# First attention of a two-layer adaLN transformer kernel: three of eight reciprocals taken within their own pair, and half the key evacuations ahead of the last exponentials

## The reference

```python
h = _layernorm(x, axis=-1) * (1 + ca) + sa
x = x + ga * _L0_attn_ref(h, ...)
# inside, 16 heads of 64: q and kv projected and rotated; keys = values = kv
lsim = einsum('bwid,bwjd->bwij', lq, _ln(lkv))   # this window of 128 tokens and the one before
gkv  = _ln(einsum('bnsd,bnsr->bnrd', segments of 16, softmax(segments @ w_proj)))
gsim = einsum('bnd,brd->bnr', q, gkv)            # pooled keys, one per segment of 16 tokens
attn = softmax(concat([gsim, lsim]), axis=-1)    # masked causally
out  = einsum('bwij,bwjd->bwid', attn, v) @ w_out + b_out
```

## Time and profile before

| | us |
|---|---|
| median of 3 runs | 1512.77 |
| the runs | 1503.08, 1512.77, 1513.02 |
| the profiled execution, its own time | 1505.21 |
| its span, first to last instruction | 1503.4 |
| mean granted TensorE clock | 0.888 |
| TensorE / VectorE / ScalarE / GpSimd busy, share of span | 79 / 63 / 55 / 48 % |

### The profile page before, as it was taken

The page is one execution under the profiler, slowest core; times in us unless marked ns, Lnnn a source line. Parts: engine busy times, 40 slices in busy tenths (PEclk is TensorE's granted clock), DMA queues, the critical chain, the costliest instruction groups (busy, mean ns, idle before and its releaser), DMA issues. The chain is left out here.

```text
span 1503.4 us, 29869 instructions
## 1 busy us (share of the span) xinstructions
PE 1185.8 (79%) x9426; PEld 935.1 (62%) x9426; DVE 944.6 (63%) x2134; ACT 826.2 (55%) x2183; POOL 727.6 (48%) x750
## 2 busy tenths in 40 slices
PE   3278989989888982898899899899937987788436
PEld 1155666656666762798899889889923444445335
DVE  4687797887887543745744664664434677777633
ACT  1256776767767772666666666666712443334101
POOL 2647558476485412565566556556644323211223
PEclk7588999899898996999999999999967998999558
DMA  6500000000000004203003000000063455331144
GB/s 185 168 3 3 2 10 3 8 5 7 10 3 8 10 8 160 92 11 126 9 11 123 14 8 10 12 9 11 10 169 86 79 84 110 60 51 21 24 125 149
DMA packets 153550, 74.98 MB, mean 50 GB/s; under 512 B 99992, under 2 KB 144408, under 8 KB 153304
## 3 DMA queue, kind: packets, MB, share of 16 engines
q1 hardware_dynamic: 145464, 64.84, 16.7%
q0 software_dynamic: 3072, 6.31, 1.3%
q10 hardware_dynamic: 4896, 2.36, 0.5%
HBM read 53.20 MB, written 19.76 MB: 49 GB/s over the span
## 5 line engine op out<-in xcount | busy, mean ns | idle before, releaser
L1495 POOL TENSOR_TENSOR hl<-hid,hh 128x256 fp32r<-128x256 f32 x396 | 293.0, 742 | 223.0 <-ACT hh L1472 218.9
L1538 DVE SCALAR_TENSOR_TENSOR hid<-GU,gub,sg 128x256 f32<-128x256 f32 x396 | 190.3, 481 | 194.6 <-ACT sg L1466 115.4
L1366 PE MATMUL GU<-xh,wh 128*128 128x256 f32 x792 | 233.4, 295 | 41.9 <-DVE wl L1514 32.7
L1466 ACT ACTIVATE sg<-GU,gub 128x256 f32<-128x256 f32 x396 | 187.8, 475 | 122.2 <-PE GU L1368 121.6
L1367 PE MATMUL GU<-xl,wh 128*128 128x256 f32 x792 | 225.2, 284 | 0.0
L1368 PE MATMUL GU<-xh,wl 128*128 128x256 f32 x792 | 225.0, 284 | 0.0
L1366 PEld LDWEIGHTS GU<-xh,wh 128*128 128x128 f32 x792 | 151.6, 191 | 52.6 <-issue 27.7
L1472 ACT CAST hh<-hid 128x256 fp32r<-128x256 f32 x396 | 158.1, 399 | 29.8 <-DVE hid L1538 28.8
L1367 PEld LDWEIGHTS GU<-xl,wh 128*128 128x128 f32 x792 | 152.0, 192 | 0.0
L1368 PEld LDWEIGHTS GU<-xh,wl 128*128 128x128 f32 x792 | 151.9, 192 | 0.0
L648 ACT ACTIVATE prob<-prob,rZ 128x272 f32<-128x272 f32 (+1 forms) x256 | 98.9, 462 | 54.0 <-DVE rZ L1029 54.0
(11 more groups left out here) (327 smaller groups left out, 2951.7 us busy)
## 6 DMA issues: line engine op xcount, KB each, us to landing
raw<-in_expert_w SPq DMA_DIRECT2D x4, 2688.0 KB, 12.2
late<-in_w SPq DMA_DIRECT2D x20, 256.0 KB, 6.2
raw<-in_expert_w SPq DMA_DIRECT2D x4, 1152.0 KB, 6.3
list<-zero SPq DMA_DIRECT2D x4, 1024.0 KB, 8.5
modb<-mod_d SPq DMA_DIRECT2D x8, 384.0 KB, 4.1
early<-rel_d SPq DMA_DIRECT2D x1, 3072.0 KB, 13.7
qkv_d<-qkv SPq DMA_DIRECT2D x48, 64.0 KB
early<-in_w SPq DMA_DIRECT2D x12, 256.0 KB, 4.3
```

What stands on the lines that cost most here:

```text
L1366: pe.matmul(out, lhs[0], rhs[0], start=start, stop=False, skip_group_check=True)
L1466: act.activation(sg[:, c % BUFS], GU[c % BUFS][:, 0:TT], ACT.Silu, bias=gub[:, GATE, e * CH0 + c:e * CH0 + c + 1]).then_inc(silu, 1)
L1495: pool.tensor_tensor(hl[:, b], hid[:, b], hh[:, b].bitcast(F32), ALU.subtract).then_inc(hid_lo, 1)
L1538: dve.scalar_tensor_tensor(out=hid[:, c % BUFS], in0=GU[c % BUFS][:, TT:2 * TT], scalar=gub[:, UP, e * CH0 + c:e * CH0 + c + 1], in1=sg[:, ...
```

## The change

VectorE's reciprocals of pairs 6, 7 and 8 no longer stand at the head of the following pair, but within their own: in pair 6 behind `kv_cosine` and ahead of the router's rows, in pair 7 between `kv_rotate` and `kv_cosine`, in pair 8 between `kv_rotate` and `kv_center` (ahead of `list_places`). Pairs 1 to 5 keep theirs where it was. Their waits (`s_exp` of the pair whose sums are read, `p_norm` for the buffer) are the same ones. On ScalarE, `keys_out(2)` and `keys_out(3)` of pair 8 come ahead of its exponentials instead of behind.

```diff
@@ ScalarE, slot_program
+                    if early and hp == 7:
+                        for c in (2, 3):
+                            keys_out(c)
                     if heads:
                         if n >= 2:
                             act.wait_ge(pT_mm, n - 1)
                         exponentials(n, hp)
-                    if early and hp == 7:
-                        for c in (2, 3):
-                            keys_out(c)
@@ VectorE, slot_program
-                    last = heads if hp > 0 else late
-                    m, pb = n - 1, (hp - 1) % 2
-                    if last:
+
+                    def reciprocals(m):
                         dve.wait_ge(s_exp, 4 * (m + 1))
                         if m >= 2:
                             dve.wait_ge(p_norm, m - 1)
-                        dve.reciprocal(rZ[:, pb], Z[:, pb]).then_inc(z_recip, 1)
+                        dve.reciprocal(rZ[:, m % 2], Z[:, m % 2]).then_inc(z_recip, 1)
+
+                    if heads and 1 <= hp <= 5:
+                        reciprocals(n - 1)
...
                     if norm and hp == 5:
                         kv_cosine(slot, r, 0)
+                    if heads and hp == 5:
+                        reciprocals(n)
...
                     if norm and hp == 6:
                         kv_rotate(r, 0)
+                    if heads and hp == 6:
+                        reciprocals(n)
+                    if norm and hp == 6:
                         kv_cosine(slot, r, 1)
                     if norm and hp == 7:
                         kv_rotate(r, 1)
+                    if heads and hp == 7:
+                        reciprocals(n)
+                    if norm and hp == 7:
                         kv_center(r, 0)
```

## The result

The changed kernel takes 1522.85 us (median of 4 runs, 1520.07 to 1525.53). The kernel before, run beside it, takes 1507.92 us (1498.25 to 1513.02). The ratio is 1.0102, interval 1.0062 to 1.0143: slower by about 15 us. The profiled execution took 1522.98 us against 1505.21, spans 1521.1 and 1503.4. The forecast of 1510.9 had the sign and the place of the slow stretch, but some 9 of the 15 us were not in its sum.

The account below looks back on a forecast made before the run. The prediction took VectorE to bound pairs 6, 7, 8 and the next slot's pair 1, with TensorE's slow scores late afterwards. Slot terms summed to +5.7 us: 1505.2 + 5.7 = 1510.9 us; range just below 1499.0 to 1522.

Parts of the forecast that it names:

- The reciprocals and the normalisations: Pairs 6 to 8: no VectorE stall; pair 8's normalisation 3 us before next maxima; ScalarE's wait 54 to about 25 us.
- a sign of being wrong: In pair 6 or 8, a reciprocal that VectorE itself waits for; slots 6 and 7 were given 0 to +1 us.
- TensorE ahead of the logits: Before the logits' transposes at a slot change, TensorE stands idle about 4.7 us.
- The length of the slow stretch: Behind that idle time, half clock until 5.1 us after the logits end; third pair's maxima 9.0 us after them.
- rival 2: Pairs 2 and 3: half clock lasts through both, +3.8 us in each of slots 3 to 6, 1527 us; chance 0.12.
- The sum by slots: First attention: slot 1 -0.1, slot 2 +2.0, slots 3 to 6 +1.1 each, slot 7 -0.6; sum +5.7 us.
- The last step: Whole kernel: 5.7 us added to the profiled execution's 1505.2 gives 1510.9; near 1518 to 1519 for a higher-group median.
- Rival 1: Behind the idle time before the logits' transposes, the clock stays at 2.4 GHz: -6.2 us, 1499.0; chance 0.25.

Follow-up runs that it names:

- e1: Changed kernel with the keys evacuated behind the eighth pair's exponentials again, so only the reciprocals move: 1505.9 us, ratio 0.9999.
- e9: Changed kernel with only the seventh pair's reciprocal put back at the head of the eighth pair: 1507.96 us, ratio 0.9991.
- e6: Changed kernel with only the eighth pair's reciprocal put back at the head of the next slot's first pair: 1527.86 us, ratio 1.0132.
- e3: Changed kernel with 20 unread matmuls ahead of TensorE's wait for the logits in slots 0 to 6: 1508.1 us, ratio 1.0013.
- e11: e7 with 6 more unread matmuls between the second pair's scores and the logits' transposes: 1501.75 us (12 runs), ratio 0.9957.
- e4: Changed kernel with the logits' transposes moved behind the second pair's scores: 1509.43 us, ratio 1.0011.
- e10: Changed kernel with the sixth and eighth pairs' reciprocals back at the head of the next pair, only the seventh's early: 1513.66 us, ratio 1.0029.
- e8: Kernel before with only the logits' transposes moved behind the second pair's scores: 1506.14 us, ratio 0.9985.
- e2: Changed kernel with all reciprocals back at the head of the next pair, so only the keys move: 1506.99 us, ratio 1.0021.
- e5: Changed kernel once more, unaltered, for a second profile: 1520.67 us, ratio 1.0088.
- e7: e4 with 12 unread matmuls ahead of the second pair's scores and 6 in the seventh pair of slot 6: 1504.95 us, ratio 0.9982.
- e12: Kernel before, unaltered, for a second profile: span 1500.1 us.

## Why the prediction missed its size

**The reciprocals and the normalisations: right.** The eighth pair's normalisation starts at 335.80, 3.2 us ahead of the maxima at 339.04 (3 predicted). ScalarE's wait for reciprocals fell from 54.0 to 21.4 us (25 predicted). In slots 1 to 5 VectorE has no new stall at a moved reciprocal, and from the seventh pair to the next slot's first its steps are those of before within 0.1 us (slot 3, whose sixth pair is late: 0.3). In slot 6 it does wait for the exponentials at them, 0.31, 0.31 and 2.35 us, which I had listed as a sign of being wrong, its cost bounded by 1 us; the next slot's first maxima weren't later for it (6.11 us behind the eighth pair's, 6.49 before).

**TensorE ahead of the logits: right.** I predicted an idle stretch of 4.7 us there; it is 4.43 or 4.44 in slots 2 to 6 and 3.26 in slot 1. The scores of the second pair were to end at L + 3.05, with L the end of the logits. L is 341.09 + 2.34 = 343.43, they end at 344.60 + 1.94 = 346.54, at L + 3.11.

**The length of the slow stretch: the term that was mis-sized.** I took it to end at L + 5.1, the mean of three spells, and said that half of the second pair's projection and values would run fast behind it, with the third pair's maxima at L + 9.0. The clock came back at 352.3, L + 8.9. Projection, values, transposes and the begin of the third pair's scores were slow, and the maxima came at L + 10.45 (353.88). That is 1.45 us more than forecast, and nearer to rival 2 (L + 11.7). Slot 1 has L + 10.46, slots 2 and 5 L + 10.93 and L + 10.92; slots 3 and 6 have L + 7.98 and L + 7.99. The row that I had for a spell at this spot, 331.09 to 341.33, was 10.24 us long; I gave it to rival 2 because no long gap stood in front of it. For slots 1, 2, 4 and 5 it was the better estimate; in slots 3 and 6 the spell behind the gap was 3.4 us, below my 5.1.

**The sum by slots.** Predicted: -0.1 for slot 1, +2.0 for slot 2, +1.1 for each of slots 3 to 6, -0.6 for slot 7; +5.7. Measured, from one slot's first maxima to the next slot's: +1.1, +2.0, +1.6, +2.1, +2.7 and +1.2 for slots 1 to 6, +0.1 for slot 7. Slot 1 itself began 0.4 us early, so that 10.4 are left. Slot 2 agrees by luck. Its third pair stood 3.9 us later behind the first than before (15.32 against 11.46), not 2.0, and 1.9 came back further on, since the kernel before had a slow spell over the sixth pair of that slot (238.9, 6.8 us; its wait was 5.14 us, now 3.05) and the changed one has not. In slots 3 and 6 the third pair wasn't late, and it was the sixth that paid (its wait was 5.00 and 5.24 us; before 3.05 and 2.73): there the short spell behind the first pair is followed by another at a gap later in the slot. The forecast had no term for that. The three slots 3 to 5, which repeat to 0.03 us, are the cleanest measure of both errors: +6.4 us (191.15 - 184.73) where the sum had +3.3.

Nor had the forecast a term for what follows the stage: in the first pair of profiles +3.2 us up to the experts and +4.1 beyond. That part isn't attributed. With the second profiles the stage alone makes up 14.3 us on average, about the whole of the 15, and 6.0 us of the changed kernel's first profile arise between 1375 and 1406 us, where its second profile loses 1.4 (see below).

**The last step.** I added 5.7 to the profiled execution's own 1505.2. The median of the four runs of the kernel before is 1507.92, which gives 1513.6 by the same sum; the median of three that I had, 1512.77, would have given 1518.5.

**What I had not seen.** The forecast explained the loss by the gap behind the first pair. e1 and, from slot 4 on, e9 have the early reciprocal of the eighth pair too, and don't even have the gap: the clock had fallen earlier, where that costs nothing, and the slow matmuls left no idle time. And e6 has the eighth pair's reciprocal late, and loses as much or more. Rival 1 had the right observation, that the 1.80 us wait at 331.47 which preceded the fall would go, and drew the wrong end from it: the fall was not saved but put off. Rule and rows: the Trainium skill, "TensorE: Matmul & The Clock Gate", section "HAM oscillation — how this bites in real kernels", says that idle time between groups of matmuls makes the next group begin cold. The rows here agree for the long gaps: behind each of the seven waits of 3.26 to 5.89 us for the logits the clock reads 0.50 when work comes back, or within 0.3 us. e3 and e11 show the other side of it, since filling the gap took the loss back (1.0013) and the fuller version went ahead of both (0.9957).

**What stays open.** Which of the gaps of 1.2 to 2.9 us bring a fall and which don't (e9 has the same two gaps with a fall and without), and what sets a spell's length. Also the end of the second attention: between 1375 and 1406 us of the kernel before, the profiles of e3, e4, e9, e10 and e11 lose 11 us against it, those of the changed kernel, e6 and e8 6.0, and e2, e5, e7 and e12 1.2 to 1.4, e1 none, whatever happened in the first attention. In e11 the clock is 0.50 there:

```profile
1375.00:1390.00 15.00, 15.00 (x85) 0.50 0.01 1
1390.00:1405.00 15.00, 10.97 (x64) 0.50 0.15 27
```

while in the kernel before it is 0.98 and 0.70:

```profile
1375.00:1390.00 15.00, 13.58 (x148) 0.98 0.23 23
1390.00:1405.00 15.00, 6.82 (x43) 0.70 0.37 49
```

This may be a large part of why single runs of every kernel here spread over 10 to 20 us; it was not tested by itself.

## What to carry to other kernels

When TensorE isn't the bound, a wait of it may cost nothing in itself, and still matter by where it lets the clock fall. Before an edit closes a wait on TensorE, look for the next place where it will idle, and whether what follows that place is hidden or on the path: here reciprocals taken earlier, together with the keys, shifted the fall by 6.8 us and cost 1%, while each half alone cost nothing that could be measured. Where a gap has to stay, matmuls that nobody reads are a cheap test, and sometimes a cure. Price a slow stretch by the spells seen at that spot, the longest as the upper bound, and not by the mean of others: here the mean of others gave +1.1 us for each of slots 3 to 6, the longest +3.8, and slots 3 to 5 took +2.1 each.

## What the hardware showed unexpectedly

- A spell at 0.50 went on for 10.2 us with TensorE busy 9.83 us of it (e9), and for 10.2 us with 8.81 (the changed kernel). The three-slot time of two profiles of one kernel agrees to 0.03 us or better, in the changed kernel even though the slot with only a short spell behind the first pair is slot 3 in one and slot 5 in the other. In both the fall's distance behind the first maxima goes 3.0 or 3.1, 4.1, 4.7 us from slot to slot and then begins again, so three slots in a row hold one of each.
- The same short idle pieces led to a fall in one slot and not in another: 1.21 and 1.42 us ahead of slot 4 of e9 did, 1.22 and 1.41 us ahead of its slot 2 did not; a single one of 1.41 us did not ahead of slots 2 to 6 of the changed kernel, and one of 1.42 us did ahead of slot 6 of e3 (449.9, for 6.8 us).
- The kernel with the highest granted clock of the first group (e3, 0.894 over its span, against 0.888 in the profile of the kernel before) was not faster than the kernel before: the mean clock says nothing of which matmuls were slow.
